# A block of state-space mixer and quantized feed-forward network: the hand-written order of steps in the mixer's turns

## The chip, the core and the metric

The kernel runs on one core of a Trainium2 chip. The metric is device time in microseconds (us), the median over runs. The core has a matrix engine (TensorE, PE in the profile; its weight loads are PEld), VectorE (DVE), ScalarE (ACT), GpSimd (POOL) and SyncE (SP), which here only issues DMAs. Each works through its own queue in order, and they wait for each other by semaphores.

## The reference

```python
h = _layernorm(x) * (1 + ca) + sa          # x: 2 x 2048 tokens x 512; modulation by the condition c
x = x + ga * attn(h)                       # the mixer
h = _layernorm(x) * (1 + cb) + sb
x = x + gb * ffn(h)                        # silu(gate) * up, then down; weights stored as integers

# the mixer
zxbcdt = u @ W_in.T                        # z 1024, xBC 1280, dt 16
dt = softplus(dt_raw + dt_bias)
xBC = silu(conv(xBC) + b_conv)             # 4 taps along the sequence, one filter a channel
Y_diag = einsum('bcln,bcsn,bhcls,bcshp->bclhp', C, B, L, X)      # within a block of tokens
states = einsum('bcln,bhcl,bclhp->bchpn', B, decay_states, X)    # carried from block to block
Y_off  = einsum('bcln,bchpn,bhcl->bclhp', C, states, state_decay_out)
y = (Y_diag + Y_off + Dp * X) * silu(z)
y = y * rsqrt(mean(y * y) + 1e-5) * norm_w
return y @ W_out.T
```

## The kernel before

The program has two parts. The mixer takes about the first 930 us and the feed-forward network the rest; only the mixer's order is changed. The mixer works in 16 turns of 256 tokens (two chunks of 128), alternating between the two sequences. Turn n runs three stages at once, for three different units of tokens: the projection, the convolution and the softplus of its own unit n (`own` in the code), the state-space part, the gating and the output projection of unit u = n - 1 (`bef`), and the layer norm of unit n + 1 (`nxt`). After the last turn a `drain` does unit 15 together with the first feed-forward tile.

Nothing schedules this at run time. For each engine the function `turn` (and `first` for turn 0, which also sets up weights and modulation) calls the steps one after another, and that is the engine's queue. The steps the text speaks of are, on TensorE: `scores_G` (L1481, C times B, the first step of a turn), `transpose_x` (L1509) and `transpose_B` (L1516), `y_off` (L1532, the carried state read through C), `y_diag` (L1544), `states` (L1557, the new state), `transpose_g` (L1572), `project_out` (L1592, L1594), `cumulate` (L1491 to L1493), and the projections `project_zdt`, `project_tile` m = 0 to 9 and `project_z` j = 0 to 3 (all L1443). Their fp32 steps go as two passes in the profile (x2 for one `y_off`). On VectorE: `conv` (L987, three taps for each of ten tiles), `softplus` s = 0 to 14, whose last result is dtA (L1038), `diff` (L1062, eight instructions a call), `scores` (L1079), `read_yoff` (L1114), `decay_S` (L1121), `read_ydiag` (L1127), `decay_X` (L1097), `gate` (L1134 to L1140), `read_state` (L1147, adds the state bank to the state tile), `low_g` (L1153), `split_h` (L975, L977). On ScalarE: `evac_*` (copies from the PSUM banks), `silu_tile` (L704, the last step of the convolution), `exp_decay` (L770), `exp_sums` (L765), `scale_out` (L788), `widen` and `measure` (L664, L671, one chunk of integer weights), `setup.read_gate_row` (L218). GpSimd multiplies the scaled output by the gate row and adds the residual (L623, L626), and makes `X * D` (L606).

Waits that matter: `y_off` of a unit's first chunk waits until `read_state` has written the last half of the unit before it. In turn 1 it waits for both gate rows too:

```python
            if u == 0 and c == 0 and f == 0:

                pe.wait_ge(setup.gate_step, 8)
                pe.wait_ge(setup.rows_read, 2)
                pe.wait_ge(setup.const_step, 11)
            if c:
                wait(pe, S_step, u, 4 * NC, 4 * c)
            else:
                wait(pe, S_step, before(u), 4 * NC, 0)
```

`scores_G` waits for all ten `silu_tile`. `cumulate` waits for dtA. The projections take turns on two PSUM banks, so each waits for the evacuation of the projection two before it.

## Time and profile before

| | us |
|---|---|
| median of 3 runs | 1459.25 (1459.07 to 1463.02) |
| the profiled execution: its time | 1463.41 |
| its span (first to last instruction) | 1461.7 |
| TensorE busy in the span | 1430.2 (98%) |
| VectorE busy | 1116.2 (76%) |
| ScalarE busy | 637.5 (44%) |
| GpSimd busy | 298.7 (20%) |
| mean granted TensorE clock | 0.996 of full speed |

A busy TensorE is one with a matmul in its pipeline, so the 98% says that it hardly stands still, and not that it works at its peak. The chain of work that ended last is made up of TensorE for 70% and of VectorE for 19%; in the mixer it changes between the two within each turn. VectorE is busy for over nine tenths of the mixer and about half of the feed-forward part.

### The profile page before, as it was taken

To read this page: it belongs to the slowest core of one execution; us is meant where nothing else is said; L and a number is where in the kernel's file an instruction comes from. 1 tells how busy PE (TensorE), PEld (TensorE's weight loads), DVE (VectorE), ACT (ScalarE), POOL (GpSimd) and SP (SyncE) were. 2 spreads that over 40 slices of the span, in tenths; PEclk is the share of its full clock that TensorE was granted. 3 is DMA by queue.
4 is the path that set the end of the run, shared out by engine and by line. 5 is a ranking of instruction groups with operands and counts; after the bars stand their busy time and mean duration, and the time that the engine had idled before them with its cause. 6 is when DMAs were issued, how large, how long until landed. Compare 5 with 4: busy or idle time off the path is not lost.

```text
span 1461.7 us, 25392 instructions
## 1 busy us (share of the span) xinstructions
PE 1430.2 (98%) x9369; PEld 1146.0 (78%) x9369; DVE 1116.2 (76%) x2521; ACT 637.5 (44%) x1300; POOL 298.7 (20%) x335
## 2 busy tenths in 40 slices
PE   7999999999999999999999999999999999999998
PEld 3677787787887887877777778779888888888887
DVE  4799998998998999999998999857536455364632
ACT  4565565575575565564655654422212011120210
POOL 1012223213212312322322132121110211101101
PEclk9999999999999999999999999999999999999999
DMA  9413213212222222132132132702210202112010
GB/s 320 151 37 131 88 45 123 87 52 96 94 88 95 68 100 95 41 135 100 39 131 81 51 116 70 292 15 80 73 59 28 87 14 73 39 49 87 8 51 30
DMA packets 56409, 124.99 MB, mean 86 GB/s; under 512 B 6438, under 2 KB 10066, under 8 KB 52188
## 3 DMA queue, kind: packets, MB, share of 16 engines
q1 hardware_dynamic: 55744, 123.27, 24.1%
q8 instruction: 77, 1.26, 0.4%
q14 instruction: 48, 0.39, 0.1%
q10 hardware_dynamic: 540, 0.07, 0.0%
HBM read 97.62 MB, written 25.69 MB: 84 GB/s over the span
## 4 chain that ended last, share of the span: by engine, by line
PE 70%; DVE 19%; issue 7%; POOL 1%; DMA 1%; ACT 1%; DVEq 0%; POOLq 0%; SPq 0%
PE bank L2032 18%; PE bank L1443 17%; PE bank L2062 9%; PE bank L1594 7%; PE bank L1592 6%; DVE xBC L987 5%; PE bank L1532 3%; DVE decay L1079 2%; PE bank L1557 2%; DVE state L1121 2%; PE bank L325 2%; DVE y L1134 1%; DVE X_D L1127 1%; PE bank L1544 1%; DVE X L1097 1%
## 5 line engine op out<-in xcount | busy, mean ns | idle before, releaser
L1867 ACT ACTIVATE silu_gate<-bank,params 128x512 f32<-128x512 f32 (+1 forms) x99 | 63.5, 642 | 366.0 <-PE bank L2032 343.8
L987 DVE SCALAR_TENSOR_TENSOR xBC<-conv_in,wconv,xBC 128x256 f32<-128x256 f32 x480 | 211.9, 474 | 3.3 <-ACT xBC L697 0.4
L1939 DVE SCALAR_TENSOR_TENSOR hidden<-bank,params,silu_gate 128x512 f32<-128x512 f32 (+1 forms) x99 | 68.3, 690 | 125.6 <-PE bank L2032 124.4
L2062 PE MATMUL bank<-W_down,hidden_high 128*128 128x512 f32 x374 | 139.1, 390 | 0.0
L606 POOL TENSOR_TENSOR X_D<-X,Drow 128x1024 f32<-128x1024 f32 x32 | 62.7, 1961 | 352.9 <-ACT X_D L781 315.5
L2032 PE MATMUL bank<-ff_h_high,W_gate 128*128 128x512 f32 (+1 forms) x352 | 132.3, 380 | 0.0
L2032 PE MATMUL bank<-ff_h_high,W_up 128*128 128x512 f32 (+1 forms) x352 | 131.1, 376 | 0.3 <-DVE hidden L1939 0.3
L2032 PE MATMUL bank<-ff_h_low,W_gate 128*128 128x512 f32 (+1 forms) x352 | 131.0, 376 | 0.0
L2032 PE MATMUL bank<-ff_h_low,W_up 128*128 128x512 f32 (+1 forms) x352 | 131.0, 376 | 0.0
L2062 PE MATMUL bank<-W_down,hidden_low 128*128 128x512 f32 x330 | 128.5, 389 | 0.0
L1443 PE MATMUL bank<-h_high,W_in_high 128*128 128x256 f32 x640 | 124.7, 317 | 0.1
L1594 PE MATMUL bank<-W_out,gT 128*128 128x512 f32 x256 | 115.0, 592 | 0.0
L1062 DVE TENSOR_SCALAR decay<-decay,sums 128x128 f32<-128x128 f32 x512 | 106.5, 283 | 0.0
L1443 PEld LDWEIGHTS bank<-h_high,W_in_high 128*128 128x128 f32 x640 | 89.0, 190 | 21.5 <-issue 18.5
L1859 POOL TENSOR_TENSOR ff_x_resid<-ff_branch,ff_x_resid 128x512 f32<-128x512 f32 x32 | 41.3, 1291 | 298.2 <-DVE ff_branch L1970 292.8
L1443 PE MATMUL bank<-h_high,W_in_low 128*128 128x256 f32 x640 | 101.5, 280 | 0.0
L1443 PE MATMUL bank<-h_low,W_in_high 128*128 128x256 f32 x640 | 101.4, 280 | 0.0
L696 ACT ACTIVATE conv_in<-bank 128x256 f32<-128x256 f32 x160 | 61.0, 381 | 88.2 <-PE bank L1443 88.2
L1970 DVE TENSOR_TENSOR ff_branch<-bank,gate_row 128x512 f32<-128x512 f32 x32 | 22.1, 690 | 100.7 <-PE bank L2062 100.7
L1544 PEld LDWEIGHTS bank<-X,decay 128*64 128x64 f32 x2048 | 65.0, 138 | 38.2 <-issue 27.7
L1079 DVE TENSOR_TENSOR decay<-decay,G_masked 128x1024 f32<-128x1024 f32 x64 | 91.9, 1436 | 0.9 <-ACT decay L770 0.4
L697 ACT ACTIVATE xBC<-bank,params,wconv 128x256 f32<-128x256 f32 x160 | 90.2, 564 | 0.0
(196 smaller groups left out, 3276.0 us busy)
## 6 DMA issues: line engine op xcount, KB each, us to landing
decay<-sums_scratch SPq DMA_DIRECT2D x32, 1024.0 KB, 5.2
wq_rows<-wqT SPq DMA_DIRECT2D x33, 256.0 KB, 4.8
widened_scratch<-wq_rows SPq DMA_DIRECT2D x33, 256.0 KB, 3.4
x_tile<-x SPq DMA_DIRECT2D x32, 256.0 KB, 3.1
x_resid<-x SPq DMA_DIRECT2D x32, 256.0 KB, 2.9
x_scratch<-x_resid SPq DMA_DIRECT2D x32, 256.0 KB, 3.0
ff_x_resid<-x_scratch SPq DMA_DIRECT2D x32, 256.0 KB, 4.5
out<-ff_x_resid SPq DMA_DIRECT2D x32, 256.0 KB, 2.0
```

The costliest lines, as they stand in the source:

```text
L697: nc.scalar.activation(A.xc[b][:, m, :], ps[:, 0:SC], ACT.Identity, bias=A.bconv[:, m:m + 1], scale=A.wconv[:, m, 3:4]).then_inc(a_emptied, 1)
L987: nc.vector.scalar_tensor_tensor(A.xc[b][:, m, :], A.raw[:, m, j:j + SC], A.wconv[:, m, j:j + 1], A.xc[b][:, m, :], ALU.mult, ALU.add).the ...
L1062: last = nc.vector.tensor_scalar(A.L[c][:, h, :], A.L[c][:, h, :], A.s3[:, c * H + h:c * H + h + 1], 0.0, ALU.subtract, ALU.min)
L1079: nc.vector.tensor_tensor(x, x, A.Gm[:, c, :].unsqueeze(1).broadcast_to([P, HH, P]), ALU.mult) \
L1443: mm = nc.tensor.matmul(out, lhs(wp, ap), rhs(wp, ap), start=(i == 0), stop=(i == last))
L1544: mm = nc.tensor.matmul(ydiag[s, h * HD:(h + 1) * HD], A.L[c][:, g, s], A.X[:, g * HD:(g + 1) * HD], start=True, stop=True, tile_position= ...
L1592: nc.tensor.matmul(ps[:], gT[gp][:, k, :], Wo[wp][:, k, :], start=(k == 0 and i == 0), stop=False)
L1594: mm = nc.tensor.matmul(ps[:], A.gT[:, k, :], A.Wo[:, k, :], start=False, stop=(k == KI - KH - 1))
L1867: self.nc.scalar.activation(B.sg[m % 2][:, 0:size], self.gates[m % 2][:, 0:size], ACT.Silu, scale=self.T.sgate[:, m:m + 1]).then_inc(self. ...
L1939: nc.vector.scalar_tensor_tensor(hid, self.ups[m % 2][:, 0:size], self.T.sup[:, m:m + 1], B.sg[m % 2][:, 0:size], ALU.mult, ALU.mult).then ...
L2032: mm = nc.tensor.matmul(ps[:, 0:self.TURNS[t][2]], W[:, k, m * P:(m + 1) * P].bitcast(dt), self.h(t, a, k).bitcast(dt), start=(k == 0 and ...
L2062: mm = nc.tensor.matmul(self.downs[c % 2][:], self.hidden_tile(t, a, m)[:, s].bitcast(dt), B.Wd[:, m, :].bitcast(dt), start=(m == 0 and a ...
```

## The change

It is one of order alone: no step is added or taken away. In `first` and in `turn`, the calls on TensorE, ScalarE and VectorE stand in another order; SyncE, GpSimd and `drain` are as before. In the set-up ahead of turn 0, TensorE does the second section of the modulation before it turns the first one's columns, and VectorE normalizes before it reads the first columns. Cut to the places that the text speaks of:

```diff
@@ -255,8 +255,8 @@
     def vector(self, dve, stats, norm, split_h):
 
         stats()
+        norm()
         self.vectors(dve, 0)
-        norm()
         self.vectors(dve, 1)
         self.low(dve, 0)
         split_h()
@@ -306,9 +306,9 @@
 
         pe.wait_ge(self.silu_c_done, 1)
         self.section(pe, 0)
+        self.section(pe, 1)
         pe.wait_ge(self.const_step, 6)
         self.turn_cols(pe, 0)
-        self.section(pe, 1)
         transpose_ln()
         self.turn_cols(pe, 1)
...
@@ -790,55 +790,55 @@
         def first():
 
             n, b = 0, 0
+            setup.exp_A(act)
+            setup.high(act, 2)
             evac_zdt(n, b, 0)
...
-            silu_tile(n, b, 3)
             evac_tile(n, b, 9)
+            silu_tile(n, b, 5)
+            setup.wout_scale(act)
             silu_z(n, 0)
-            silu_q(n, b)
-            silu_tile(n, b, 4)
             setup.wout_hi(act)
+            setup.read_gate_row(act, 0)
+            silu_tile(n, b, 6)
+            silu_z(n, 1)
             measure(n, 0)
-            silu_tile(n, b, 5)
-            silu_z(n, 1)
-            setup.wout_scale(act)
-            silu_tile(n, b, 6)
+            silu_tile(n, b, 7)
             evac_ln(after(n), 1 - b, n)
-            setup.read_gate_row(act, 0)
-            silu_tile(n, b, 7)
-            widen_second(n)
             silu_z(n, 2)
             silu_tile(n, b, 8)
+            silu_z(n, 3)
             silu_tile(n, b, 9)
+            exp_decay(n, 0, 0)
+            widen_second(n)
+            exp_decay(n, 0, 1)
             setup.read_gate_row(act, 1)
-            silu_z(n, 3)
             exp_sums(n)
-            exp_decay(n, 0, 0)
-            exp_decay(n, 0, 1)
             exp_decay(n, 1, 0)
             exp_decay(n, 1, 1)
             measure_second(n)
...
@@ -848,74 +848,68 @@
             own, bef, nxt = has_own(n), has_before(n), has_next(n)
             if bef:
                 evac_x(n, u, 0)
+                evac_B(n, u, 0)
             if own:
                 evac_zdt(n, b, 0)
                 evac_zdt(n, b, 1)
-                widen_extra(n)
-                exp_dt(n)
                 evac_tile(n, b, 0)
                 evac_tile(n, b, 1)
+                exp_dt(n)
+                widen_extra(n)
                 evac_tile(n, b, 2)
-            if bef:
-                evac_B(n, u, 0)
-            if own:
-                silu_q(n, b)
                 evac_tile(n, b, 3)
                 evac_tile(n, b, 4)
+            if bef:
...
+                silu_z(n, 1)
                 measure(n, 0)
-                silu_tile(n, b, 3)
-                silu_z(n, 1)
             if bef:
                 evac_g(n, u, 1)
-            if own:
-                silu_tile(n, b, 4)
+                square(u, 1)
+            if own:
+                silu_tile(n, b, 5)
+                silu_tile(n, b, 6)
+                silu_tile(n, b, 7)
                 silu_z(n, 2)
-            if bef:
-                square(u, 1)
-            if own:
-                silu_tile(n, b, 5)
-                widen_second(n)
             if nxt:
                 evac_ln(after(n), 1 - b, n)
             if own:
-                silu_tile(n, b, 6)
-                silu_tile(n, b, 7)
+                widen_second(n)
                 silu_z(n, 3)
                 silu_tile(n, b, 8)
                 silu_tile(n, b, 9)
                 exp_decay(n, 0, 0)
-                exp_sums(n)
             if bef:
                 scale_out(n, u, 1)
             if own:
                 exp_decay(n, 0, 1)
                 measure_second(n)
+                exp_sums(n)
                 exp_decay(n, 1, 0)
                 exp_decay(n, 1, 1)
...
+            conv(n, b, 3, 2)
+            if own:
                 softplus(n, 10)
+                conv(n, b, 2, 1)
+            if bef:
+                low_g(n, u, 0)
+            if own:
                 softplus(n, 11)
-            if bef:
-                low_g(n, u, 0)
-            if own:
+                conv(n, b, 5, 0)
                 softplus(n, 12)
+                softplus(n, 13)
+                conv(n, b, 2, 2)
+                softplus(n, 14)
             if bef:
                 scores(u, 1, 1)
...
+            if bef:
+                read_yoff(n, u, b, 1, 1)
             if own:
                 conv(n, b, 6, 2)
-                sums(n)
-                conv(n, b, 7, 2)
-            if bef:
-                read_yoff(n, u, b, 1, 1)
-                decay_S(u, b, 1, 1)
+            if bef:
                 read_ydiag(u, 1, 1)
                 decay_X(n, u, 1)
+            if own:
+                conv(n, b, 9, 0)
+            if bef:
                 gate(n, u, b, 1)
+            if own:
+                conv(n, b, 8, 0)
             if nxt:
                 norm(after(n), n, 0)
-            if own:
-                conv(n, b, 8, 0)
-                conv(n, b, 8, 1)
+            if bef:
+                decay_S(u, b, 1, 1)
             if nxt:
                 norm(after(n), n, 1)
             if own:
@@ -1350,8 +1355,7 @@
             if bef:
                 low_g(n, u, 1)
             if own:
-                conv(n, b, 9, 0)
-                conv(n, b, 8, 2)
+                conv(n, b, 8, 1)
             if bef:
                 read_state(u, b, 1, 0)
             if own:
@@ -1359,16 +1363,19 @@
                 diff(n, 0, 0)
                 diff(n, 0, 1)
                 conv(n, b, 9, 2)
+                conv(n, b, 8, 2)
                 diff(n, 1, 0)
-            if bef:
-                read_state(u, b, 1, 1)
+                diff(n, 1, 1)
             if nxt:
                 split_h(after(n), n, 0)
+            if own:
+                tails(n, b)
+            if nxt:
                 split_h(after(n), n, 1)
             if own:
-                tails(n, b)
                 exact_flag(n)
-                diff(n, 1, 1)
+            if bef:
+                read_state(u, b, 1, 1)
 
...
@@ -1597,67 +1604,67 @@
         def first():
 
             n, b = 0, 0
+            setup.turn_params(pe)
             project_zdt(n, 0)
             project_zdt(n, 1)
             pe.wait_ge(setup.win_low, 2)
             project_tile(n, 0)
-            setup.turn_params(pe)
             project_tile(n, 1)
+            project_tile(n, 2)
             setup.section(pe, 2)
-            project_tile(n, 2)
             setup.section(pe, 3)
             setup.turn_cols(pe, 2)
             project_tile(n, 3)
-            setup.section(pe, 4)
             project_tile(n, 4)
             setup.turn_cols(pe, 3)
+            setup.section(pe, 4)
             pe.wait_ge(setup.win_low, 3)
             project_tile(n, 5)
             project_tile(n, 6)
+            cumulate(n)
             project_tile(n, 7)
-            cumulate(n)
             project_tile(n, 8)
             setup.section(pe, 5)
+            project_tile(n, 9)
             setup.turn_cols(pe, 4)
-            project_tile(n, 9)
+            setup.gate_rows(pe)
+            setup.turn_cols(pe, 5)
             pe.wait_ge(setup.win_low, len(setup.stage))
             project_z(n, 0)
-            setup.turn_cols(pe, 5)
             project_z(n, 1)
+            transpose_ln(after(n), n)
             project_z(n, 2)
-            setup.gate_rows(pe)
             project_z(n, 3)
-            transpose_ln(after(n), n)
 
         def turn(n, b):
             u = before(n)
             own, bef, nxt = has_own(n), has_before(n), has_next(n)
             if bef:
                 scores_G(n, u, b)
+                transpose_x(n, u, b, 0)
+                y_off(u, b, 0, 0)
             if own:
                 project_zdt(n, 0)
-            if bef:
-                y_off(u, b, 0, 0)
-                transpose_x(n, u, b, 0)
-            if own:
                 project_zdt(n, 1)
             if bef:
+                transpose_B(n, u, b, 0)
                 y_off(u, b, 0, 1)
+            if own:
+                project_tile(n, 0)
+            if bef:
                 y_diag(n, u, 0, 0)
             if own:
-                project_tile(n, 0)
                 project_tile(n, 1)
             if bef:
                 y_diag(n, u, 0, 1)
             if own:
                 project_tile(n, 2)
             if bef:
-                transpose_B(n, u, b, 0)
+                transpose_x(n, u, b, 1)
             if own:
                 project_tile(n, 3)
             if bef:
                 states(n, u, 0, 0)
-                transpose_x(n, u, b, 1)
             if own:
                 project_tile(n, 4)
             if bef:
@@ -1672,18 +1679,18 @@
                 transpose_g(n, u, 0)
             if own:
                 project_tile(n, 7)
+                project_tile(n, 8)
+            if bef:
+                y_diag(n, u, 1, 0)
+            if own:
+                cumulate(n)
             if bef:
                 y_off(u, b, 1, 0)
-                y_diag(n, u, 1, 0)
-            if own:
-                cumulate(n)
-                project_tile(n, 8)
-            if bef:
                 project_out(n, u, 0)
+                y_off(u, b, 1, 1)
             if own:
                 project_tile(n, 9)
             if bef:
-                y_off(u, b, 1, 1)
                 y_diag(n, u, 1, 1)
             if own:
                 project_z(n, 0)
@@ -1699,8 +1706,8 @@
             if own:
                 project_z(n, 3)
             if bef:
+                project_out(n, u, 1)
                 states(n, u, 1, 1)
-                project_out(n, u, 1)
```

How the rows of the queues stand now, at three places. On TensorE, the border between two later turns, before (the last step is the last part of the output projection, L1594; the next turn begins at L1481):

```order
L1594 MATMUL bank<-W_out,gT 128x512 x4
L1481 MATMUL bank<-xBC 128x128 x2
L1443 MATMUL bank<-W_in_high,h_high 128x272 x4
L1443 MATMUL bank<-W_in_high,h_low 128x272 x4
L1443 MATMUL bank<-W_in_low,h_high 128x272 x4
L1532 MATMUL bank<-state,xBC 128x512
L1509 MATMUL bank<-ident,xBC 128x128 x8
L1443 MATMUL bank<-W_in_high,h_high 128x272 x4
L1443 MATMUL bank<-W_in_high,h_low 128x272 x4
```

and now (seven lines are added ahead of these functions, so L1481 is L1488, L1532 is L1539 and so on):

```order
L1601 MATMUL bank<-W_out,gT 128x512 x4
L1564 MATMUL bank<-X,B_rows 128x512
L1488 MATMUL bank<-xBC 128x128 x2
L1516 MATMUL bank<-ident,xBC 128x128 x8
L1539 MATMUL bank<-state,xBC 128x512
L1450 MATMUL bank<-W_in_high,h_high 128x272 x4
L1450 MATMUL bank<-W_in_high,h_low 128x272 x4
L1450 MATMUL bank<-W_in_low,h_high 128x272 x4
```

The second half of `states` (L1557, now L1564) has moved behind the output projection to the end of the turn, and the transposes of x and the first `y_off` ahead of the first projection of the next turn.

On VectorE, whose lines stand six lower in the changed file, the same border, before (L1147 is `read_state`, L1070 the first step of the next turn):

```order
L1062 TENSOR_SCALAR decay<-decay,sums 128x128 x8
L1147 TENSOR_TENSOR state<-bank,state 128x512
L975 CAST h_high<-X_D 128x4x128
L977 TENSOR_TENSOR h_low<-X_D,h_high 128x4x128
L975 CAST h_high<-X_D 128x4x128
L977 TENSOR_TENSOR h_low<-X_D,h_high 128x4x128
L997 COPY conv_tail<-conv_in 128x30
L998 COPY conv_in<-conv_tail 128x10x3
L1062 TENSOR_SCALAR decay<-decay,sums 128x128 x8
L1070 TENSOR_TENSOR G_masked<-bank,triu 128x256
```

and now:

```order
L981 SCALAR_TENSOR_TENSOR xBC<-conv_in,wconv,xBC 128x256 x2
L1056 TENSOR_SCALAR decay<-decay,sums 128x128 x16
L969 CAST h_high<-X_D 128x4x128
L971 TENSOR_TENSOR h_low<-X_D,h_high 128x4x128
L991 COPY conv_tail<-conv_in 128x30
L992 COPY conv_in<-conv_tail 128x10x3
L969 CAST h_high<-X_D 128x4x128
L971 TENSOR_TENSOR h_low<-X_D,h_high 128x4x128
L1141 TENSOR_TENSOR state<-bank,state 128x512
L1064 TENSOR_TENSOR G_masked<-bank,triu 128x256
```

The last `read_state` has moved behind `split_h` to the very end, and the last eight `diff` ahead of `split_h`.

On ScalarE, the end of turn 0, before (from `evac_ln` to the last `measure` of the turn):

```order
L656 ACTIVATE X_D<-bank,modc 128x256 x4
L218 ACTIVATE gate_row<-bank 128x512
L704 ACTIVATE xBC<-xBC 128x256
L664 ACTIVATE wq_rows<-wq_rows 128x512
L712 ACTIVATE silu_z<-bank 128x512
L704 ACTIVATE xBC<-xBC 128x256 x2
L218 ACTIVATE gate_row<-bank 128x512
L712 ACTIVATE silu_z<-bank 128x256
L765 ACT_TABLE_LOAD
L765 ACTIVATE exp_sums<-sums 128x96
L770 ACTIVATE decay<-decay 128x1024 x4
L671 ACTIVATE wq_rows,wq_squares<-wq_rows 128x512
```

and now:

```order
L656 ACTIVATE X_D<-bank,modc 128x256 x4
L712 ACTIVATE silu_z<-bank 128x512
L704 ACTIVATE xBC<-xBC 128x256
L712 ACTIVATE silu_z<-bank 128x256
L704 ACTIVATE xBC<-xBC 128x256
L770 ACT_TABLE_LOAD
L770 ACTIVATE decay<-decay 128x1024
L664 ACTIVATE wq_rows<-wq_rows 128x512
L770 ACTIVATE decay<-decay 128x1024
L218 ACTIVATE gate_row<-bank 128x512
L765 ACTIVATE exp_sums<-sums 128x96
L770 ACTIVATE decay<-decay 128x1024 x2
```

The last two `silu_tile` stand ahead of the second gate row, and that one behind a table load, two `exp_decay` and a `widen`.

## Rows read from the trace of the kernel before

**Rows 1.** Windows view, one later turn: length, then busy us (instructions) of PE, PEld, DVE, ACT, POOL, granted clock, DMA share, GB/s.
```profile
133.00:189.00 56.00, 55.83 (x429) 44.48 (x428) 52.00 (x126) 33.02 (x71) 13.96 (x14) 1.00 0.25 86
```

**Rows 2.** Line view of L1481, TensorE: durations in ns, start us of turns 2, 14 and 15.
```profile
L1481 PE MATMUL bank<-xBC x4: 272/275/276, 133.1 to 133.4; 128*128 128x128 f32 x4
...
L1481 PE MATMUL bank<-xBC x4: 272/276/276, 811.2 to 811.6; 128*128 128x128 f32 x4
...
L1481 PE MATMUL bank<-xBC x4: 272/274/276, 869.2 to 869.5; 128*128 128x128 f32 x4
```

**Rows 3.** Waits view, TensorE, whole program: us in total, times, longest.
```profile
PE bank L1491 <- DVE dtA L1038: 2.6, 15, 0.2
PE bank L1557 <- DVE state L1147: 2.4, 6, 0.5
```

**Rows 4.** Timeline, TensorE, first stage: start, us, instruction, count, [idle before <-releaser].
```profile
12.06 0.38 PE L339 MATMUL bank<-ident,gT 2*128 2x2 f32 x4 [0.77 <-ACT gT L195]
...
20.82 1.25 PE L1443 MATMUL bank<-W_in_high,h_high 128*128 128x272 f32 x4 [3.50 <-DVE h_low L977]
...
28.37 0.64 PE L351 MATMUL bank<-ident,X 10*128 10x10 f32 x4
```

**Rows 5.** Timeline, TensorE, end of the first turn and head of turn 1.
```profile
69.51 1.04 PE L1433 MATMUL bank<-ident,x_tile 128*128 128x128 f32 x8
74.53 1.03 PE L1481 MATMUL bank<-xBC 128*128 128x128 f32 x4 [3.99 <-ACT xBC L704]
...
81.37 1.02 PE L1532 MATMUL bank<-state,xBC 128*128 128x512 f32 x2
```

**Rows 6.** Timeline, ScalarE, end of the first turn.
```profile
74.35 0.62 ACT L218 ACTIVATE gate_row<-bank 128x512 f32<-128x512 f32 x1
...
75.26 1.28 ACT L765 ACT_TABLE_LOAD   x1
...
76.74 3.88 ACT L770 ACTIVATE decay<-decay 128x1024 f32<-128x1024 f32 x4
```

**Rows 7.** Windows view as in rows 1, after the first long TensorE wait.
```profile
20.80:21.80 1.00, 0.98 (x4) 1.00 (x5) 0.96 (x2) 0.92 (x1) 0.00 (x0) 0.50 1.04 382
```

**Rows 8.** Timeline, TensorE, head of turn 7, a steady one.
```profile
415.25 0.61 PE L1481 MATMUL bank<-xBC 128*128 128x128 f32 x4
415.61 0.75 PE L1443 MATMUL bank<-W_in_high,h_high 128*128 128x272 f32 x4
...
417.20 1.02 PE L1532 MATMUL bank<-state,xBC 128*128 128x512 f32 x2
418.06 1.04 PE L1509 MATMUL bank<-ident,xBC 128*128 128x128 f32 x8
418.86 0.74 PE L1443 MATMUL bank<-W_in_high,h_high 128*128 128x272 f32 x4
...
420.43 1.02 PE L1532 MATMUL bank<-state,xBC 128*128 128x512 f32 x2
```

**Rows 9.** Timeline, GpSimd and VectorE, where both work on SBUF tiles.
```profile
416.22 1.29 POOL L623 TENSOR_TENSOR branch<-branch,gate_row 128x512 f32<-128x512 f32 x1 [7.36 <-ACT branch L788]
...
416.35 2.23 DVE L1079 TENSOR_TENSOR decay<-decay,G_masked 128x1024 f32<-128x1024 f32 x1
...
424.57 1.22 DVE L1079 TENSOR_TENSOR decay<-decay,G_masked 128x1024 f32<-128x1024 f32 x1
...
466.66 1.65 DVE L1062 TENSOR_SCALAR decay<-decay,sums 128x128 f32<-128x128 f32 x8
...
811.30 3.88 DVE L1062 TENSOR_SCALAR decay<-decay,sums 128x128 f32<-128x128 f32 x8
```

**Rows 10.** Timeline, VectorE, last third of turn 7.
```profile
453.91 0.68 DVE L1127 TENSOR_TENSOR X_D<-bank,X_D 128x512 f32<-128x512 f32 x1
...
460.73 0.69 DVE L1153 TENSOR_TENSOR gT_low<-bank,gT_high 128x512 fp32r<-128x512 f32 x1 [0.71 <-ACT gT_high L751]
...
470.56 0.69 DVE L977 TENSOR_TENSOR h_low<-X_D,h_high 128x512 fp32r<-128x512 f32 x1
```

178 lines of the change are left out of this document (91 added, 87 removed).

## The prediction

> **What bounds the kernel now.** I read the windows view first. In a later turn, 133 to 189 us, TensorE is busy for 55.8 of 56 us and VectorE for 52.0 of 56 [rows 1]. So TensorE sets the pace, and VectorE has about 4 us a turn to lose before it sets it instead. ScalarE with 33 us has room, but its steps stand in a queue too. The starts of `scores_G`, the first step of every turn, give the length of a turn: (811.2 - 133.1) / 12 = 56.5 us for turns 2 to 13, and 58.0 us for turn 14 [rows 2].
>
> The waits view tells what a better order could give back in the turns. TensorE waits 15 times for dtA, 2.6 us in all, and 6 times for `read_state` ahead of the second half of `states`, 2.4 us in all [rows 3]. That is 5.0 us. Turn 14 is 58.0 - 56.5 = 1.5 us longer than the mean of the others. Its cause is in the trace: eight `diff` on VectorE took 3.88 us [rows 9], where eight `diff` elsewhere take 1.65 [rows 9], and `y_off` came late.
>
> In the first stage there is more in one piece: TensorE waits 0.77 us for a read of the modulation, 3.50 us for the first h_low, and at the end of turn 0 3.99 us for the last `silu_tile` [rows 4, 5]. After the first long wait the granted clock is 0.50 [rows 7], that is 1.2 GHz and not 2.4. After the second the steps from `scores_G` to the second `y_off` take 81.37 - 74.53 = 6.84 us, where a steady turn has 420.43 - 415.25 = 5.18 for them [rows 5, 8]: the same fall, for 1.7 us.
>
> **The set-up and turn 0.** Section 1 of the modulation now runs while ScalarE reads section 0, so the 0.77 us go. `turn_params` (28.18 to 28.94, of which 0.64 us are the last four instructions [rows 4]) moves into the wait for h_low, which hides it: 0.76 us more. From there to the end of `project_z` 3 TensorE had no wait before, and I find none now: the tiles are the same, and the modulation's sections have landed. `transpose_ln` now stands ahead of the last two `project_z`, for 0.87 us. So the last projection ends at 69.51 - 0.77 - 0.76 + 0.87 = 68.9 us instead of 69.5, and `evac_ln`, which ScalarE could only begin at 70.15, runs under them. What ScalarE has left at 68.9 is two `silu_z` and two `silu_tile`: the last ends near 70.3, and `scores_G` starts there, 4.2 us before the 74.53 of before [rows 5].
>
> But this is given back in part. `y_off` now comes before the projections, and in turn 1 it waits for the second gate row. ScalarE's order puts ahead of that row a table load of 1.28 us, two `exp_decay` of 3.88 / 4 = 0.97 each, and a `widen`, which I take like the row itself at about 0.5 [rows 6]: 70.3 + 1.28 + 1.94 + 0.5 + 0.5 = 74.5 us. From one `y_off` to the next, with two projections between, the steady turn needs those 5.2 us less `scores_G` (415.61 - 415.25 = 0.36) and the transposes (418.86 - 418.06 = 0.80), so 4.0 [rows 8]. The second `y_off` then starts at 78.5 us, against 81.37 before [rows 5]: **2.9 us gained**, if the clock stays up.
>
> Does it? TensorE would be idle from 68.9 to 70.3, busy for 1.2 us, and idle from 71.5 to 74.5, 3.0 us. No run here shows such a pair. Gaps of 0.77 us left the clock up, gaps of 3.50 and 3.99 took it down [rows 4, 5], and 3.0 is nearer to the latter. Its price was 1.7 us after the wait at 74.53 (above), and I take it in full: the start is then worth 2.9 - 1.7 = **1.2 us**, with 2.9 as its other end. It could be 0 if ScalarE is late by another 1.2.
>
> **The later turns.** TensorE does the same steps, and its pairs of neighbours are alike in kind, so its own work keeps its length; I bound the change of the seams by 0.2 us a turn either way and take 0. What counts is who is late.
>
> (a) dtA: `scores` for the last heads (1.22 us [rows 9]) now comes after the last `softplus` on VectorE and not before it, so dtA is due 1.2 us earlier. But ScalarE's silu table load (1.28 us, as in rows 6) now falls between tile 5 and tile 6, right ahead of the copy that `low_g` waits for, and `low_g` is in front of dtA. I expect a fifth of the 2.6 us to stay.
>
> (b) `read_state` for the first half: its second `states` now comes after `project_tile` 4 as before, but VectorE has put fewer convolutions ahead of `gate`. By VectorE's durations it is ready about 0.6 us early. The 2.4 us go.
>
> (c) The new wait: `states` is the last step of the turn. It needs 0.86 us to the next start (like `y_off`, 418.06 - 417.20), its result is there 1.02 us after its start [rows 8], so 0.16 us into the next turn. `read_state` takes 0.68, like the read of the same shape in [rows 10], so the state is ready at 0.04 + 0.16 + 0.68 = 0.9 us. `y_off` is due after `scores_G` and the transposes, at 0.36 + 0.80 = 1.16 us. So it fits, with 0.3 us to spare, if VectorE is free at 0.2 us. Queued behind it on TensorE is the whole next turn.
>
> (d) Is it free? The last thing that VectorE gets from TensorE is `y_diag`. In turn 7 `read_ydiag` started at 453.91, that is 38.7 us into the turn (415.25); it could have started at 38.1, when the product was there, and with the wait for dtA gone it starts at 37.9. From there to the last h_low VectorE took 470.56 - 453.91 = 16.65 us, of which 0.71 was a wait [rows 10]. To this the new order adds a `decay_S` (0.6), eight `diff` (1.6) and the tails (0.2), and takes away `read_state` (0.6) and small pauses (0.2): 16.65 - 0.71 + 1.6 = 17.5. The last h_low starts at 37.9 + 17.5 = 55.4 and ends at 56.1 of a turn of 56.1. VectorE is just in time, by 0.1 us for `read_state` and 0.3 more for `y_off`. I take no wait.
>
> So of the 5.0 us 4.5 go, and turn 14's 1.5 too, since its cause was a meeting of GpSimd with `diff` that now stand elsewhere: **6.0 us**, bounds 0 and 7.5.
>
> **The drain.** Its first step is `y_off`, which had no wait since `read_state` was long done. Now it comes right after `states`, and must wait the 0.9 us of (c), behind the flag work that stands ahead of `read_state` in turn 15. Lost: **1.0 us**, between 0.9 and 2.
>
> **Sum.** 1.2 + 6.0 - 1.0 = 6.2 us of the profiled execution's 1463.4, which lies 4.2 above the median of 1459.25; both fall alike. I predict 1453, own range 1449 to 1457.
>
> **The rivals.**
>
> *GpSimd locks VectorE out (slower).* Rows 9 show it: at 416.35 `scores` took 2.23 us while GpSimd multiplied by the gate row (416.22, 1.29 us), and 1.22 when GpSimd was idle. VectorE waited for GpSimd to end. That multiplication follows the end of the output projection, and so comes 0.86 us earlier in the new order: 416.22 - 415.25 - 0.86 = 0.1 us after the turn's start. VectorE's last h_low (0.69 us, two inputs in SBUF) is due from 55.4 to 56.1, so right before. If VectorE is 0.7 us late it meets the multiplication, waits for its end at 0.1 + 1.3 = 1.4 us, ends h_low at 2.1 and `read_state` at 2.8, and `y_off` starts 1.7 us late. That is decided anew in every turn, from 0.7 us of lateness on: 14 turns x 1.7 = 24 us, less the 6.2: 1477. For it: VectorE has no slack to speak of in (d). Against it: I counted the waits that I could see. Chance 0.12. The Trainium skill, page "SBUF — State Buffer", section "SBUF: two separate sides", says that the port pair which VectorE and GpSimd share is an exclusive lock, held for the whole instruction, also against a VectorE operation with two SBUF inputs. By that rule the trace agrees (2.23 against 1.22 us), and the price is the whole 1.7 us and not a share of it.
>
> *VectorE becomes the pace.* It loses more than its 4 us a turn in new waits: for `y_off`, `y_diag`, `low_g`. Then the turns stay at 56.5 us, the 6.0 become about 0.5, and the start and the drain cancel: 1459, range 1457 to 1461. For it: 52.0 of 56 busy. Chance 0.23.
>
> *The start keeps its clock and all waits go.* 2.9 + 6.5 - 1.0 = 8.4, and up to 0.2 us in each of 14 turns at the seams: 1448, range 1444 to 1449. Chance 0.10.
>
> *The order isn't what limits.* If TensorE's waits only move elsewhere in the turn, as in a ring they may, the time stays: this has the same time as the second rival and is counted there.
>
> **How the numbers follow.** The forecast has 0.55 and gives 1453. 0.3% of the time is 4.4 us, about what a measurement can tell from no change, so faster is under 1454.9 and slower over 1463.6. Of the forecast I count 0.45 as faster and 0.10 as the same; with 0.10 of the third rival and 0.05 for the lower edge of the second, faster is 0.60. Same is 0.10 + 0.16 = 0.26. Slower is the lock with 0.12 and 0.02 of the second rival: 0.14. The range of 8 in 10 holds the forecast, the second rival and most of the third: 1446 to 1461, and leaves out the lock.
>
> **What would show each step.** Right: `scores_G` of turn 1 near 70.3 us and `y_off` behind it near 74.5, with a wait for gate_row; `scores_G` of turn 2 near 129.5 us; turns of 56.0 to 56.2 us; no wait of `states` for `read_state`. The clock after 74.5 us is 0.50 for some 3 us, or it isn't. Wrong: a wait of `y_off` for `read_state` at the head of every turn, 0.1 to 0.6 us if VectorE is merely late and about 1.7 if GpSimd holds it; an h_low or a cast of much over 0.7 us beside L623. If the turns are 56.5 us with VectorE's waits gone, VectorE has the pace.

## The result, and the profile of the kernel after

The new order is slower. The kernel after takes 1475.51 us in the median (1470.41 to 1477.58), the kernel before 1462.13 us measured beside it (1459.07 to 1463.02). The ratio is 1.0089, with a 95% interval of 1.0064 to 1.0115. The prediction was 1453, faster, with a range up to 1461.

The profiled execution of after took 1471.67 us, with a span of 1469.8 us, so 8.1 us more than the span before (1461.7). It is one of the faster executions of after, and the one of before (1463.41) is slower than all five of its median, so the traces show 8.1 of the 13.4 us between the medians. The starts of `scores_G` divide it up. In the kernel after this step is L1488, and its rows at the heads of turns 1, 2, 14 and 15 and in the drain are, from the timeline of TensorE (start, us, instruction):

```profile
69.81 0.71 PE L1488 MATMUL bank<-xBC 128*128 128x128 f32 x4 [1.81 <-ACT xBC L704]
...
130.96 0.61 PE L1488 MATMUL bank<-xBC 128*128 128x128 f32 x4
...
818.15 0.61 PE L1488 MATMUL bank<-xBC 128*128 128x128 f32 x4
...
874.80 0.61 PE L1488 MATMUL bank<-xBC 128*128 128x128 f32 x4
...
935.03 0.61 PE L1488 MATMUL bank<-xBC 128*128 128x128 f32 x4
```

Against [rows 2], turn 2 starts 2.1 us earlier (131.0 for 133.1). Turns 2 to 13 take (818.15 - 130.96) / 12 = 57.27 us each where they took 56.5, which is 9.1 us in all. Turn 14 takes 56.65 us for 58.0. Turn 15 takes 60.2 us, 2.2 more than before. The rest is as long as it was, within 0.3 us. The sum is -2.1 + 9.1 - 1.3 + 2.2 + 0.3 = 8.2 us, the 8.1 of the spans but for rounding. So the question is what happens in turns 2 to 13.

The windows view of one later turn, from its start on, answers to [rows 1]. Its columns are the same: length, busy us and instructions of PE, PEld, DVE, ACT and POOL, granted clock, DMA share, GB/s.

```profile
131.00:187.00 56.00, 55.92 (x428) 44.61 (x427) 51.94 (x125) 32.42 (x70) 13.49 (x14) 1.00 0.26 86
```

That looks like [rows 1]: a turn without a mishap is no different, and nobody works longer. The turns are not alike, though. In the trace they are 56.2 to 58.5 us long, where before eight of these twelve were under 56.6. What TensorE waits for in them is in the waits view (us in total, times, longest), from 131 to 811 us:

```profile
PE bank L1440 <- ACT gT L756: 4.6, 7, 1.4
PE bank L1498 <- DVE dtA L1032: 1.3, 2, 0.7
PE bank L1579 <- DVE y L1134: 1.0, 5, 0.2
```

The waits of [rows 3] are nearly gone: dtA is 1.3 us in two turns, and `states` waits for nothing. But there is a wait that wasn't there before. `transpose_ln` (L1440) finds its PSUM bank taken, since ScalarE hasn't copied gT out of it (L756).

### The profile page after: what moved, and what is told of

It reads as the page before. It is cut to its first block and busy times, and to the rows that moved or that the text cites. A ratio compares the mean times of both kernels' runs of the same rounds, so it can differ in the third digit from the quotient of the medians.

```text
span 1469.8 us, 25393 instructions
## 1 busy us (share of the span) xinstructions
PE 1435.1 (98%) x9369; PEld 1149.8 (78%) x9369; DVE 1123.3 (76%) x2521; ACT 640.8 (44%) x1300; POOL 287.1 (20%) x335
## 5 line engine op out<-in xcount | busy, mean ns | idle before, releaser
L981 DVE SCALAR_TENSOR_TENSOR xBC<-conv_in,wconv,xBC 128x256 f32<-128x256 f32 x480 | 254.1, 551 | 3.3 <-ACT xBC L697 3.1
L606 POOL TENSOR_TENSOR X_D<-X,Drow 128x1024 f32<-128x1024 f32 x32 | 62.6, 1956 | 384.2 <-ACT X_D L781 340.4
L2039 PE MATMUL bank<-ff_h_low,W_gate 128*128 128x512 f32 (+1 forms) x352 | 131.0, 376 | 0.0
L1450 PE MATMUL bank<-h_high,W_in_high 128*128 128x256 f32 x640 | 130.2, 325 | 0.4 <-ACT z_dt L720 0.4
L1056 DVE TENSOR_SCALAR decay<-decay,sums 128x128 f32<-128x128 f32 x512 | 103.2, 276 | 0.9 <-DMA decay<-sums_scratch 0.9
L1450 PE MATMUL bank<-W_in_high,h_high 128*128 128x272 f32 (+2 forms) x384 | 87.8, 351 | 1.1 <-DVE h_low L971 1.1
L1601 PEld LDWEIGHTS bank<-W_out,gT 128*128 128x128 f32 x256 | 48.5, 189 | 48.8 <-issue 46.0
```

The lines of the kernel that those rows point to most:

```text
L606: nc.gpsimd.tensor_tensor(A.XD[:].rearrange("p (h d) -> p h d", h=H), A.X[:].rearrange("p (h d) -> p h d", h=H), A.Drow[:].unsqueeze(2).br ...
L981: nc.vector.scalar_tensor_tensor(A.xc[b][:, m, :], A.raw[:, m, j:j + SC], A.wconv[:, m, j:j + 1], A.xc[b][:, m, :], ALU.mult, ALU.add).the ...
L1056: last = nc.vector.tensor_scalar(A.L[c][:, h, :], A.L[c][:, h, :], A.s3[:, c * H + h:c * H + h + 1], 0.0, ALU.subtract, ALU.min)
L1450: mm = nc.tensor.matmul(out, lhs(wp, ap), rhs(wp, ap), start=(i == 0), stop=(i == last))
L1601: mm = nc.tensor.matmul(ps[:], A.gT[:, k, :], A.Wo[:, k, :], start=False, stop=(k == KI - KH - 1))
L2039: mm = nc.tensor.matmul(ps[:, 0:self.TURNS[t][2]], W[:, k, m * P:(m + 1) * P].bitcast(dt), self.h(t, a, k).bitcast(dt), start=(k == 0 and ...
```

## Where the time goes: one turn followed back

I follow that wait back in turn 7, which starts at 417.56 us and is 57.6 us long. ScalarE's timeline:

```profile
460.14 0.38 ACT L712 ACTIVATE silu_z<-bank 128x256 f32<-128x256 f32 x1 [0.20 <-PE bank L1450]
462.75 0.63 ACT L671 ACTIVATE wq_rows<-wq_rows 128x512 f32<-128x512 f32 x1 [2.22 <-DMA widened_scratch<-wq_rows]
463.28 0.19 ACT L671 ACTIVATION_READ_ACCUMULATOR wq_rows<-wq_rows 128x1 f32 x1
463.38 0.58 ACT L751 ACTIVATE gT_high<-bank 128x512 fp32r<-128x512 f32 x1
464.79 0.60 ACT L756 ACTIVATE gT<-bank 128x512 f32<-128x512 f32 x1 [0.84 <-DVE gT_low L1147]
```

`measure` (L671) squares a chunk of integer weights and has nothing to do with the turn. It waits 2.22 us until SyncE's store of that chunk has landed, and `evac_g` (L751, L756), on which VectorE's `low_g` and TensorE's bank depend, stands right behind it. Why is the store late? SyncE's timeline of the same turn (the time at the left is that of issue):

```profile
453.56 0.33 SPq L539 DMA_DIRECT2D sums_scratch<-sumsT  x1
456.10 0.33 SPq L548 DMA_DIRECT2D decay<-sums_scratch  x1
456.48 0.42 SPq L510 DMA_DIRECT2D widened_scratch<-wq_rows  x1
456.95 0.58 SPq L565 DMA_DIRECT2D x_scratch<-x_resid  x1
```

SyncE first stores the sums of dtA (L539, 16 KB), waits until they have landed, broadcasts them back (L548, 1024 KB), and only then issues the store of the weights (L510, 256 KB). So the store is queued behind a result of VectorE, the step `sums`: three short instructions that copy what `cumulate` has made. In that turn VectorE had them ready at 453.5 us. Its timeline, and GpSimd's:

```profile
445.10 2.52 DVE L981 SCALAR_TENSOR_TENSOR xBC<-conv_in,wconv,xBC 128x256 f32<-128x256 f32 x2
447.55 0.68 DVE L1108 TENSOR_TENSOR y<-bank,exp_sums 128x512 f32<-128x512 f32 x1
448.15 0.68 DVE L952 BATCH_NORM_STATS2 bn_stats<-x_tile 128x6 f32<-128x512 f32 x1
...
452.90 0.21 DVE L1043 COPY sums<-bank 128x64 f32<-128x64 f32 x1
453.15 0.19 DVE L1045 TENSOR_TENSOR sums<-sums 128x32 f32<-128x32 f32 x1
453.26 0.27 DVE L1047 COPY sumsT<-bank 32x128 f32<-32x128 f32 x1
453.46 1.32 DVE L981 SCALAR_TENSOR_TENSOR xBC<-conv_in,wconv,xBC 128x256 f32<-128x256 f32 x1
```

```profile
445.36 1.99 POOL L606 TENSOR_TENSOR X_D<-X,Drow 128x1024 f32<-128x1024 f32 x1 [20.66 <-ACT X_D L781]
...
453.16 1.34 POOL L623 TENSOR_TENSOR branch<-branch,gate_row 128x512 f32<-128x512 f32 x1 [2.94 <-ACT branch L788]
```

The first row holds `conv` 4, 0 and `conv` 5, 1. Two convolutions elsewhere take some 0.9 us; these two take 2.52. GpSimd's multiplication by D runs from 445.36 to 447.35. The first convolution began 0.26 us before it and was not touched. The second came after its start and ended at 447.62, just after the multiplication. In the kernel before, what stood there on VectorE was a read of PSUM and a `decay_S`, which took 1.19 us for 0.68 elsewhere, and the sums were ready at 34.2 us of the turn. Turn 7 of before, VectorE and GpSimd:

```profile
442.89 0.69 DVE L1114 TENSOR_TENSOR y<-bank,exp_sums 128x512 f32<-128x512 f32 x1
443.50 1.19 DVE L1121 TENSOR_TENSOR state<-state,exp_sums 128x512 f32<-128x512 f32 x1
```

```profile
442.24 1.91 POOL L606 TENSOR_TENSOR X_D<-X,Drow 128x1024 f32<-128x1024 f32 x1 [19.66 <-ACT X_D L781]
```

Now they are ready at 35.9 or 36.0 us in eight of the 15 turns. In five others they also meet GpSimd's multiplication by the gate row (L623), which starts within 0.01 us of the difference of two sums (L1045), and then they are ready at 37.1 to 37.7. (In turn 1, which is longer at its start, they are ready at 40.8.) With the sums at 37.1 or later, turns 2 to 14 took 57.5 to 58.5 us, with the sums at 35.9 or 36.0 they took 56.3 to 57.6. In one turn alone, turn 4, the convolution had started just ahead of GpSimd: the sums were ready at 34.6 us, and that turn took 56.2 us.

What sorts the turns without an exception is the start of `measure`, that is the landing of the store (us from the turn's start, in the trace of after):

| turn | sums ready | `measure` starts | length of the turn |
|---|---|---|---|
| 4 | 34.6 | 42.80 | 56.21 |
| 8 | 35.9 | 43.75 | 56.32 |
| 14 | 35.9 | 44.27 | 56.65 |
| 7 | 36.0 | 45.19 | 57.58 |
| 10 | 37.1 | 46.14 | 58.52 |

From 43.9 us on (11 of the turns 2 to 14) the turn ends 12.39 us after the start of `measure`, to within 0.01 us. The sums are not all that moves that start: their own small store (L539) took 1.4 us until the broadcast could be issued in turn 8, and 2.5 us in turn 7.

The Trainium skill, page "SBUF — State Buffer", section "SBUF: two separate sides", says that a VectorE operation with two SBUF inputs and a GpSimd operation that reads SBUF exclude each other for the whole instruction, and that whichever starts first has the port pair. The trace agrees with both halves: 2.13 us for the convolution that came second, 0.48 for the one that came first. That GpSimd waited in its turn is not shown: its multiplication took 2.10 us in turn 4 and 1.98 elsewhere.

So the chain is: GpSimd's multiplication, `conv` 5, 1, the sums, SyncE's queue, the store, `measure`, `evac_g`, and then both `transpose_ln` and VectorE's last third. I call this theory M. The rival, theory V, is the second one of the prediction: VectorE has too much to do, and the waits only show where it is late.

## The experiments

The times are compared with runs of the kernel before on the same chip: its median was 1460.6 us beside e1 to e4, 1461.2 beside e5 to e8 and 1460.6 beside e9 to e12. After was not run again beside them, where before was 0.9 to 1.6 us faster than in the result above, so what is said below to be gained over after may be too large by as much. The `...` in the diffs stands for calls left out.

**e1: ScalarE copies gT ahead of the measuring.**

```diff
                 silu_z(n, 1)
-                measure(n, 0)
+            if own and n == N - 1:
+                measure(n, 0)
             if bef:
                 evac_g(n, u, 1)
                 square(u, 1)
+            if own and n != N - 1:
+                measure(n, 0)
```

> The kernel after, with one thing changed on ScalarE: in the later turns measure(n, 0), which waits for a DMA store, stands behind evac_g(n, u, 1) and square(u, 1) and not ahead of them (in turn 15 it stays where it is, since the flags there need it). Theory M (the wait for the store holds up the copy of gT, and that the transposes): the waits of transpose_ln for gT (4.6 us in turns 2 to 13) and the later states, cumulate and project_z that come of them go, turns of 56.2 to 56.6 us in the place of 57.3, so about 8 us less than the kernel after: 1467 us, 1.003 of before. Theory V (VectorE itself has too much to do, since GpSimd now meets its convolutions: 631.4 us busy against 623.5): the waits only change their names, the turns keep 57.0 us or more, 1472 to 1476 us.

Measured: 1469.08 us, 1.0052 of before (1.0033 to 1.0070). That is 6.4 us less than after, and the wait for gT is gone. So ScalarE's order carries a part, as theory M says, but not all. This is what remains of TensorE's waits from 131 to 816 us:

```profile
PE bank L1602 <- ACT silu_z L712: 2.2, 11, 0.2
PE bank L1501 <- DVE dtA L1035: 1.3, 2, 0.7
PE bank L1582 <- DVE y L1137: 1.3, 6, 0.2
PE bank L1526 <- ACT X L736: 0.4, 1, 0.4
```

`measure` now comes after `square`, and `silu_z` behind it is what TensorE waits for; and the sums are still late. The experiment took away a little under half of the loss against before (a ratio of 1.0052 for 1.0089) and moved a part of it within ScalarE's queue; what the rest is it does not tell.

The 631.4 and 623.5 us of VectorE in the expectation are of windows of 687 and 678 us. Over the same 678 us it was busy for 622.5 us in after and 623.5 in before, so they say nothing for theory V.

**e2: the sums earlier on VectorE.**

```diff
                 conv(n, b, 5, 2)
                 conv(n, b, 4, 1)
+                sums(n)
                 conv(n, b, 7, 0)
                 conv(n, b, 4, 2)
...
                 conv(n, b, 7, 2)
-                sums(n)
                 conv(n, b, 6, 1)
```

> The kernel after, with sums(n) on VectorE in the later turns moved four steps of convolutions and one read and scale earlier, from behind conv 7, 2 to behind conv 4, 1 (some 3 us earlier in the turn, about where the kernel before has it). Nothing else. SyncE stores the sums, broadcasts them and only then issues the store that measure(n, 0) waits for. Theory M with this as its origin: the store is issued near 37.5 us of the turn and not 39.7, ScalarE finds it done at 43 us, the waits for gT go, 7 to 9 us less: 1467 us. Theory V: nothing of it changes, 1474 us. If the store is late for another reason than its issue (contention among the transfers), its issue moves and its landing does not: 1472 to 1476 us with the waits left.

Measured: 1457.40 us, 0.9979 of before (0.9969 to 0.9988). One step of 0.6 us, moved 3 us ahead in its queue, takes off 18 us, twice what theory M expected, and makes the new order faster than the old. TensorE's waits from 131 to 811 us are down to one line:

```profile
PE bank L1498 <- DVE dtA L1032: 1.3, 2, 0.7
```

In turn 7 (from 412.24) the sums leave at 32.8 us, and the store of the weights now waits for ScalarE's widening alone:

```profile
445.02 0.32 SPq L539 DMA_DIRECT2D sums_scratch<-sumsT  x1
446.43 0.33 SPq L548 DMA_DIRECT2D decay<-sums_scratch  x1
448.25 0.32 SPq L510 DMA_DIRECT2D widened_scratch<-wq_rows  x1
```

Theory V falls. The convolution still meets GpSimd here (a mean `conv` of 538 ns from 133 to 811 us, with 553 in after and 474 in before), VectorE is busy for 623.6 of these 678 us, with 622.5 in after, and TensorE doesn't wait for it but for the 1.3 us above.

**e3 and e4: the two halves of the change.** e3 has the set-up and first turn of after and the later turns of before; e4 the reverse.

> The set-up and first turn of the kernel after, the later turns of the kernel before. The start's share by itself. By my count of the start (2.1 us earlier at the second turn in the trace of after), 1460 us, that is 2 us under before (0.9985); the clock may fall or not after the last silu of turn 0, which is worth 1.5 us either way. If the start owes its gain to the new order of the later turns, 1462.

> The set-up and first turn of the kernel before, the later turns of the kernel after. If the loss is all in the later turns: turns of 57.3 us as in the kernel after, 2 us more than the kernel after, so 1476 to 1479 us, 1.010 to 1.012 of before. If the new first turn leaves a lateness that the ring of later turns carries on: about 1466 us.

Measured: e3 1458.0 us, 0.9979 (0.9968 to 0.9990); e4 1473.62 us, 1.0078 (1.0049 to 1.0106). The start is worth 2.6 us by itself, and the loss is in the later turns whatever comes before them. By the expectation e4 should have come out 2 us over after; it is 1.9 under, which its interval of 4 us either way allows for. In e4 the wait for gT is 7.3 us in 8 turns.

**e5: the store ahead of the sums on SyncE.** VectorE's late sums stay.

```diff
                 load_wq(n, 0)
+                if has_before(n):
+                    store_wq(n, 0)
 
                 wait(sp, sums_step, n, 3, 3)
...
                     if c == 0:
-                        store_wq(n, 0)
+                        if not has_before(n):
+                            store_wq(n, 0)
```

> The kernel after, with one issue moved on SyncE in the later turns: store_wq(n, 0) stands ahead of the wait for the sums and not behind the first broadcast of the sums. VectorE's order, with its late sums, stays as in after. In e2 both the store and the broadcast came earlier; here only the store does, so this tells the two apart. If the late store is all (ScalarE's measure waits for it, and evac_g behind it): the store is issued near 36.0 us of the turn, measure starts at 42.8 us in every turn, turns of 56.2 us, 1457 to 1459 us as with e2. If the late broadcast and what else hangs on the late sums count too: better than e1 (1469) by little, 1464 to 1469 us. If the late issue isn't the point: 1474.

Measured: 1461.32 us, 1.0002 (0.9990 to 1.0014), so 14 of e2's 18 us, by the store alone. `measure` starts at 42.8 us in the later turns, with no wait. The remaining 4 us were in neither the first nor the last case of the expectation but between. By the trace of e5 they are the other effect of the late sums on VectorE's own queue: the sums are ready at 35.9 or 37.1 us, `gate` behind them ends at 43.2 or 43.5 us instead of 42.8, and in the turns with 43.5 `transpose_g` waits 0.2 us for it. The DMA views of turn 7 show the size of the transfer's part. In after (456 to 463 us) the store was issued 0.4 us behind the broadcast, in e5 (449 to 457 us) ahead of it; the last number is us from issue to landing:

```profile
decay<-sums_scratch SPq DMA_DIRECT2D x1, 1024.0 KB, 6.0
widened_scratch<-wq_rows SPq DMA_DIRECT2D x1, 256.0 KB, 6.2
```

```profile
decay<-sums_scratch SPq DMA_DIRECT2D x1, 1024.0 KB, 5.1
widened_scratch<-wq_rows SPq DMA_DIRECT2D x1, 256.0 KB, 2.8
```

So the store lost twice: in turn 7 it was issued 2.9 us later than in e5, and took 3.4 us longer.

**e6: GpSimd's multiplication cut short.** The second multiplication by D of each turn is done for 4 of the 32 heads; the products of the others are left out of the result.

```diff
+            hs = H // 8 if c else H
-            nc.gpsimd.tensor_tensor(A.XD[:].rearrange("p (h d) -> p h d", h=H),
+            nc.gpsimd.tensor_tensor(A.XD[:].rearrange("p (h d) -> p h d", h=H)[:, 0:hs, :],
...
```

> The kernel after, with GpSimd's second multiplication by Drow in each turn (times_D for chunk 1) done for 4 of the 32 heads alone; the output lacks the other products, and VectorE's work is the same. This takes away the meeting of that multiplication with conv 7, 0 (2.13 us in the place of 0.48). Theory L (the meeting with GpSimd is what makes the sums late): the sums are ready at 34.6 us in every turn, as by chance in turn 4 of the profile of after, not at 35.9 or 37.1; all turns 56.2 us; 1458 to 1461 us. Theory O (the place of the sums in VectorE's order is enough by itself, the meeting adds little): sums at 34.6 us but the store still late, turns of 56.7 us and more, 1465 to 1470 us. No effect: 1474.

Measured: 1457.36 us, 0.9976 (0.9967 to 0.9986), the same as e2. The sums are ready at 34.6 us with VectorE's order untouched. Theory L holds: the order alone would have had the sums in time. It is the meeting, 1.65 us longer for one convolution, that put them beyond the point.

**e9: the meeting avoided, with all work done.** Left out work could act in another way, so the same was tried by order. `conv` 5, 1 goes behind the statistics and the read of PSUM, and these two also change places with each other.

```diff
                 conv(n, b, 4, 0)
-                conv(n, b, 5, 1)
-            if bef:
-                read_yoff(n, u, b, 1, 0)
             if nxt:
                 stats(after(n), 1)
+            if bef:
+                read_yoff(n, u, b, 1, 0)
             if own:
+                conv(n, b, 5, 1)
                 conv(n, b, 5, 2)
```

> The kernel after, with conv 5, 1 on VectorE in the later turns moved two steps later, behind stats(after(n), 1) and the read of the first y_off of chunk 1; nothing else, and all work is done. In after conv 5, 1 came 0.15 us after the start of GpSimd's multiplication by Drow and took 2.13 us. The statistics and the read of PSUM don't seem to be held up by GpSimd in the trace, so they should now fill that time. Theory L (the meeting is what tips the sums over): conv 5, 1 takes under 0.8 us, the sums are ready at 34.6 us of the turn instead of 35.9 or 37.1, turns of 56.2 us, 1457 to 1460 us, like e6 where GpSimd's work was left out. If the statistics or the read are held up as well: sums at 35.9 and 1472 to 1476 us.

Measured: 1457.89 us, 0.9984 (0.9975 to 0.9993). VectorE and GpSimd in turn 7:

```profile
439.83 0.47 DVE L981 SCALAR_TENSOR_TENSOR xBC<-conv_in,wconv,xBC 128x256 f32<-128x256 f32 x1
440.23 0.68 DVE L952 BATCH_NORM_STATS2 bn_stats<-x_tile 128x6 f32<-128x512 f32 x1
440.94 0.18 DVE L954 BATCH_NORM_AGGREGATE mean_var<-bn_stats 128x2 f32<-128x6 f32 x1
441.12 0.69 DVE L1108 TENSOR_TENSOR y<-bank,exp_sums 128x512 f32<-128x512 f32 x1
441.73 3.12 DVE L981 SCALAR_TENSOR_TENSOR xBC<-conv_in,wconv,xBC 128x256 f32<-128x256 f32 x7
```

```profile
440.09 1.98 POOL L606 TENSOR_TENSOR X_D<-X,Drow 128x1024 f32<-128x1024 f32 x1 [20.84 <-ACT X_D L781]
```

The statistics and the read of PSUM run beside the multiplication at 0.68 and 0.69 us, as long as anywhere. The seven convolutions after them take 3.12 us. The sums are ready at 34.7 us. This change of three neighbouring calls is worth 17.6 us.

**e10: how late is too late.** The sums one convolution earlier than in after, 0.4 us.

```diff
+                sums(n)
                 conv(n, b, 7, 2)
-                sums(n)
```

> The kernel after, with the sums one convolution earlier (ahead of conv 7, 2, 0.4 us). A point between after (ready at 35.9 or 37.1 us of the turn, 1475 us) and e6 (34.6, 1457 us). If the loss grows evenly with the lateness of the sums: 35.5 us, 1466 to 1470 us. If a second meeting matters, that of the sums with GpSimd's multiplication by the gate row, which starts at 35.56 us: at 35.5 it is just dodged, the sums never come at 37.1, and the time is 1463 to 1466 us. If that meeting still happens in many turns: 1472 us.

Measured: 1463.55 us, 1.0022 (1.0013 to 1.0031). The sums are ready at 35.5 us, and they just miss GpSimd's second multiplication, which cuts off the 37.1 us of after. The points so far, ready time in the turn against time: 32.8 and 34.6 us give 1457, 35.5 gives 1463.6, and 35.9 to 37.7 gives 1475.5. It is a flat stretch and then a slope. The start of `measure` shows the bend in single turns of e10: five of the turns 2 to 14 have it by 43.7 us and are 56.2 us long, or 56.25, and where it is 44.4 or later the turn ends 12.39 us behind it, as in after. (Turn 4 has it at 42.8, turn 6 at 44.2.) The sums were ready at 35.5 or 35.6 us in nearly all of them; what differs is how long the two stores behind them took. So late sums bring the turn to the bend, near 43.8 us for `measure`, and the transfers decide how far it goes past it.

**e7 and e12: the same in the old order.** e7 is the kernel before with the sums moved behind the last read of `y_off`. e12 is e7 with the store ahead, as in e5.

```diff
                 conv(n, b, 6, 2)
-                sums(n)
                 conv(n, b, 7, 2)
             if bef:
                 read_yoff(n, u, b, 1, 1)
+            if own:
+                sums(n)
+            if bef:
                 decay_S(u, b, 1, 1)
```

> The kernel before, with the sums of the later turns on VectorE moved behind conv 7, 2 and the read of the second y_off of chunk 1, that is from an end at 34.2 us of the turn to one near 38.4. All else as before. If late sums are the cause, whatever the rest of the order: measure, which before found the store landed at 42 to 43.7 us, waits until about 46.5 us, gT and the transposes with it, turns of 58 us or more: 1480 to 1500 us. If the late sums hurt only in the new order: within 3 us of before.

> The kernel of e7 (before with sums 4.3 us later, 1525.6 us) with the store on SyncE ahead of the wait for the sums, as in e5. If nearly all of e7's 64 us came by way of the store and measure: 1463 to 1475 us. If the late broadcast (diff on VectorE needs it) carries a large part at this lateness: 1480 to 1510 us. If the store isn't on the path: 1525.

Measured: e7 1525.6 us, 1.0438 (1.0413 to 1.0462); e12 1490.37 us, 1.0195 (1.0178 to 1.0212). The sums are ready at 38.4 to 39.5 us of the turn, and the old order loses more than the new: 64 us, above the range that I gave. The waits view of e7, TensorE, whole program:

```profile
PE bank L1435 <- ACT gT L756: 37.2, 14, 3.5
```

It is the same line as in after, eight times as large. With the store ahead (e12) 35 of the 64 us are gone. They are not the wait alone, for in e7, with waits for gT of up to 3.5 us, the clock fell too. One of the stretches, in the windows view of e7:

```profile
488.00:494.00 6.00, 5.09 (x21) 4.66 (x22) 6.00 (x26) 4.41 (x10) 0.88 (x2) 0.50 0.65 260
```

The mean granted clock is 0.981 in e7's trace, and 0.996 in those of before and e12. An estimate from these: 0.019 x 1524 - 0.004 x 1462 = 23 us of full clock lost in e7 beyond what before loses, and none of it in e12; it is an upper bound, since a lower clock costs time only where TensorE has the pace. So the 64 us are a wait and a fall of the clock together, and the size of e7's loss is not what late sums cost while the clock stays up, as it did in after (0.997). In e12 the rest shows as waits of VectorE for the broadcast itself:

```profile
DVE decay L1065 <- DMA decay<-sums_scratch: 12.1, 10, 2.0
```

This second way was not seen in after. That it carries all of the other 29 us was not tested.

**e8 and e11: a version that beats both.** e8 is e2, with ScalarE's read of the second gate row ahead of the first `exp_decay` in turn 0, and with `states` ahead of the last `project_out` in turn 15. e11 moves VectorE's last `read_state` of turn 15 ahead of `split_h` as well.

```diff
+            setup.read_gate_row(act, 1)
             exp_decay(n, 0, 0)
             widen_second(n)
             exp_decay(n, 0, 1)
-            setup.read_gate_row(act, 1)
```

> The kernel of e2 (after with early sums), with two more edits: in the first turn ScalarE reads the second gate row ahead of the first two exp_decay and the widening, not behind them, and in turn 15 states for the last half stands ahead of the second output projection again, as in before. By the first, y_off of turn 1 is due at 71.8 us and not 74.1, and if the shorter gap keeps the clock up, 1.5 us more: 2.3 to 3.8 us. By the second, the wait of y_off at the start of the drain (1.6 us and the seams, 2.2 in all) goes. From 1457.4: 1451 to 1453 us, 0.994 of before. If the gap ahead of y_off still takes the clock down: 1453 to 1454.

> The kernel of e8 with the last read_state of turn 15 on VectorE ahead of split_h and the flag work. In e8 states had been moved ahead in turn 15 and y_off of the drain still started 58.7 us after the turn's start, since this read came last in VectorE's queue. If that is the cause: y_off at 57.9 us, 0.6 to 0.8 us under e8: 1455 us, 0.9955 of before. If something else holds y_off: as e8, 1455.9.

Measured: e8 1455.94 us, 0.9963 (0.9951 to 0.9975), the fastest kernel of this study, 19.6 us under after; its interval overlaps with that of e2 (0.9969 to 0.9988), so what it adds to e2 is not clear of noise. e11 1456.46 us, 0.9969 (0.9959 to 0.9979), no different. In e8's trace turn 2 starts at 128.6 us, where e2's starts at 130.6, so not the hoped-for 3.8 us earlier. Nor is it shown that the gate row gave these 2.0: e10, which has the start of after unchanged, begins turn 2 at 128.8 us in its trace. What holds e8 there is not the clock. e11 has the same start, its granted clock is 1.00 from 70 to 82 us, and its turn 2 starts at 128.6 us too. TensorE, in e11 from 66 to 82 us:

```profile
PE bank L1525 <- ACT X L736: 2.1, 1, 2.1
```

It is `transpose_B` of turn 1, which waits for ScalarE's copy of the transposed x (L736), and that stands behind four `exp_decay` and a `measure` of turn 0. It starts at 77.5 us in e8 and at 77.6 in e11. What an earlier `y_off` gains is given back in this wait.

The edits of turn 15 went at the wrong wait. With e8's the turn took 58.8 us, with 58.7 in e2. The 58.7 us that the expectation of e11 gives for the drain's `y_off` are those of `scores_G` behind it; `y_off` started 57.8 us after the turn's start in e2 and in e8, and in e11, whose edit was to bring it forward, at 58.4. What it waits for is shown below, with the drain: a flag that VectorE writes, and that e11's edit put 0.6 us later.

## The prediction, step by step

**The start: right, and its size nearly.** [rows 5] gave 81.37 us for the second `y_off`; I took off 1.2 us. The rows of after:

```profile
74.33 1.10 PE L1539 MATMUL bank<-state,xBC 128*128 128x512 f32 x2 [2.93 <-ACT gate_row L218]
...
79.91 1.02 PE L1539 MATMUL bank<-state,xBC 128*128 128x512 f32 x2
```

The gain is 81.37 - 79.91 = 1.5 us. `scores_G` started at 69.8 (70.3 was predicted), `y_off` at 74.3 (74.5), after a wait of 2.9 us (3.0) for the gate row. The clock fell, as I took it to: the window behind the wait has a granted clock of 0.65. e3 measured the start by itself at 2.6 us. The other end of the prediction occurs too: in e10, with the same start, the clock fell behind the first of the two waits and was up again at `y_off` (1.00 from 73.8 to 78.0 us), and the second `y_off` started at 77.8 us, 3.5 us earlier than in before.

```profile
74.30:78.70 4.40, 4.37 (x19) 3.92 (x20) 2.40 (x3) 3.42 (x6) 0.90 (x1) 0.65 0.74 223
```

**(a), (b) and turn 14: right in kind; (c) by luck.** The waits for dtA fell from 2.6 to 1.3 us, in two turns, and not to a fifth, those for `read_state` went, and `y_off` at the head of the turn has no new wait. For (c) that is luck, since its wait does not exist, though the description of the kernel above has it too. `wait(pe, S_step, before(u), 4 * NC, 0)` counts the steps of the units ahead of `before(u)`, so `y_off` needs the state of unit u - 2, the last one of its own sequence, and not that of the unit just before it, as I took it. The trace of after agrees: the drain's `y_off` started at 934.10 us, and the last `read_state` (L1141) at 935.31. Turn 14 got its 1.3 us back. But the size of what they could bring was too large: in e2, where nothing else is in the way, turns 2 to 13 take (806.32 - 130.62) / 12 = 56.31 us, for the 56.5 of before, and not the 56.0 to 56.2 that I named. Most single waits for dtA were 0.2 us, and a quiet turn of the new order is as long as a quiet turn of the old. So the seams that I set to 0 seem to have taken back what those waits gave; no run takes the two apart. So the 6.0 us were rather 2.4 + 1.7 = 4.1 us.

**(d): the step that failed.** I listed what VectorE has from `read_ydiag` on, and asked whether its last h_low is in time. I set no price on the moved `sums`, and did not follow who waits for them. The answer stands on two queues of engines that the diff doesn't touch, SyncE's and GpSimd's. SyncE holds the weight store behind the sums, and ScalarE's `measure` holds `evac_g` behind the store. In the kernel before this had little to spare already: ScalarE waited there too, 7.9 us in six turns (24.8 us in 14 in after), but not right ahead of `evac_g`, since two other steps stood between. The term "later turns, +6.0" was in fact -9.1 + 1.3 = -7.8 us in the profiled execution, and the runs put nearly all of it, 14 to 18 us against e5 and e2, on this chain.

**The rival of the lock: its mechanism was right, its place and its way to the end were not.** I put it at the head of the turn, at `h_low` against L623, with 1.7 us a turn, from 0.7 us of lateness on. The meeting that counts is 28 us into the turn, `conv` against L606, and it costs TensorE nothing there. The way that I gave it, from `h_low` over `read_state` to `y_off`, leads nowhere, by (c) above. The meeting costs by making a 16 KB result late for a queue. That the rival's 1477 us came near 1475.5 is a coincidence of sizes. [rows 9] had shown how one such meeting looks; what I left undone was to lay the new order of VectorE against GpSimd's times for the whole turn. It would have shown L606 over two convolutions, where before it lay over a PSUM read and half a `decay_S`.

**"VectorE becomes the pace": wrong.** Its waits went with the sums (e2), though its work didn't change.

**The drain: right in sign by luck.** 1.0 us was predicted, for a wait of `y_off` for `read_state`. Turn 15 took 2.2 us more, and `y_off` did wait:

```profile
934.10 1.10 PE L1539 MATMUL bank<-state,xBC 128*128 128x512 f32 x2 [1.63 <-issue]
```

But it cannot have waited for `read_state`, which started behind it. The other step that TensorE does here is to read the flag by which the feed-forward part chooses its number format; VectorE had written it at 932.80 to 932.94 us. The source view of after has this read, and the tile view of the flag names `y_off` as what waited for it, 1.6 us:

```profile
L2026 PEldq TENSOR_LOAD <-wide_flag x1: 492/492/492, 933.0 to 933.0; - x1
```

In each of the ten traces in which `y_off` waits here, it starts 1.15 to 1.20 us after the end of the flag's instruction. In before the flag ended 1.51 us ahead of `y_off` and TensorE was still at its output projection, so nothing was lost. In the new order the last `diff` stand ahead of the flag on VectorE and `read_state` behind it: the flag starts 55.5 us into the turn in before, 56.5 in e2 and 58.0 in after. So the new order costs 0.7 us here (turn 15 takes 58.7 us in e2, e6 and e9, for 58.0), and the other 1.5 us of after came with the late sums. In e11 `read_state` stands ahead of the flag again, which starts at 57.1 us.

## To carry to other kernels

When a step moves, follow its result through the queues of all engines, those that issue DMAs above all: a result of a few kilobytes can hold up a large transfer that has nothing to do with it, and that one can hold up the critical engine two queues further on. Lay the new order of VectorE against the times of GpSimd's long multiplications, and put there what the traces show unharmed beside them: a read of PSUM (0.69 us) or the statistics (0.68). A single SBUF tensor as input is not enough: of the `diff` of turn 14 in before, two took 1.41 and 1.38 us for 0.28, beside L623 and L626. A step that waits for a DMA belongs behind the steps that others wait for, not ahead of them. And read a wait from its count in the code: `before(u)` with a count of 0 was the state of two units ago.

## What the hardware showed that I had not expected

A 256 KB store took 6.2 us to land when it was issued 0.4 us behind a 1024 KB broadcast from the same queue, and 2.8 us when issued ahead of it. The Trainium skill, page "DMA: Bandwidth & Descriptors", section "Queues, rings and completion order", says that each DMA engine takes a ring's descriptors in their order; the two numbers agree with that.

Which of two engines waits at a meeting was decided by 0.1 us and less. In turn 4 of after `conv` 5, 1 started 0.14 us ahead of GpSimd's multiplication and took 0.48 us; in each of the other 14 turns a convolution started 0.14 us behind it and took 2.12 to 2.13 us. The difference of two small sums (L1045) takes 0.19 us. In nine turns of after it started 0.001 to 0.006 us ahead of L623 and took that; in five turns it started 0.007 to 0.011 us behind L623 and took 1.33 us.

The clock did not fall after every wait of the same length. `scores_G` of turn 1 waited 1.8 us in after, e8, e10 and e11. Behind it the granted clock was 1.00 in after (69.7 to 71.7 us) and in e11, 0.56 in e8 (69.9 to 73.1 us) and 0.53 in e10 (69.3 to 71.3 us). After and e10 have the same start, and so have e8 and e11, so it is not the order that decides. What does stays open.

```profile
69.70:71.70 2.00, 1.59 (x12) 1.35 (x12) 2.00 (x4) 1.97 (x3) 0.00 (x0) 1.00 0.00 0
```

```profile
69.90:73.10 3.20, 3.17 (x13) 2.76 (x14) 3.17 (x6) 3.17 (x4) 0.00 (x0) 0.56 0.02 5
```
